# Spreading a row to all partitions through DRAM, and sixteen graphs written out, in a four-layer graph network on one core

## The reference, cut to what matters

```python
z = x @ W.T + bW
ai, aj = z @ wai + bai, z @ waj + baj          # one number for each node
e = ai + transpose(aj)                         # 1024 x 1024
e = where(e >= 0, e, 0.2 * e)
att = softmax(where(adjs > 0, e, -9e15) with a sink column of -1e9)[:, :n]
x = layernorm(x + att @ z)
```

## Time and profile before

| | |
|---|---|
| median of three executions | 3152.99 us |
| the profiled execution | 3149.12 us |
| its span, first to last instruction | 3147.0 us |
| PE busy (matmul) | 2898.2 us, 92% |
| DVE busy | 2090.7 us, 66% |
| ACT busy | 1324.8 us, 42% |
| POOL busy | 928.0 us, 29% |
| mean granted TensorE clock | 0.978 of full speed |

### The profile page before, as it was taken

The page is one execution under the profiler, slowest core; times in us unless marked ns, Lnnn a source line. Parts: engine busy times, 40 slices in busy tenths (PEclk is TensorE's granted clock), DMA queues, the critical chain, the costliest instruction groups (busy, mean ns, idle before and its releaser), DMA issues.

```text
span 3147.0 us, 45004 instructions
## 1 busy us (share of the span) xinstructions
PE 2898.2 (92%) x14794; PEld 2444.4 (78%) x14794; DVE 2090.7 (66%) x4724; ACT 1324.8 (42%) x2468; POOL 928.0 (29%) x1088
## 2 busy tenths in 40 slices
PE   4729999999999999999999999999999999999997
PEld 4618878887888878887888888888788878888886
DVE  3277677585867768585776758676676857677533
ACT  0232535435352533535253443526344362535423
POOL 1112332242233224232333323233332422332230
PEclk8969999999999999999999999999999999999998
DMA  4023040301304030120403012040302203040100
GB/s 130 19 89 100 1 134 1 108 28 41 94 1 134 1 108 27 44 91 1 134 1 115 20 50 86 5 130 1 122 14 71 64 13 123 1 134 1 37 18 14
DMA packets 203486, 181.41 MB, mean 58 GB/s; under 512 B 15568, under 2 KB 184944, under 8 KB 203248
## 3 DMA queue, kind: packets, MB, share of 16 engines
q1 hardware_dynamic: 62560, 109.94, 10.3%
q10 hardware_dynamic: 140688, 68.46, 7.8%
HBM read 161.17 MB, written 17.19 MB: 57 GB/s over the span
## 4 chain that ended last, share of the span: by engine, by line
PE 65%; issue 13%; DVE 7%; DMA 4%; POOL 3%; ACT 2%; SPq 1%; POOLq 0%; DVEq 0%; ACTq 0%
PE bank L716 18%; PE bank L732 16%; PE bank L673 8%; PE bank L675 8%; PE bank L674 8%; PE bank L632 2%; DMA adj_col<-in_adj 2%; PE bank L641 2%; DMA x_even<-in_x 2%; POOL rstd L1009 1%; DVE hid L1237 1%; DVE stat L1145 1%; PE bank L753 1%; PE bank L652 1%; POOL adj_col L1031 1%
## 5 line engine op out<-in xcount | busy, mean ns | idle before, releaser
L732 PE MATMUL bank<-W,hid 128*128 128x256 f32 x3072 | 696.7, 381 | 15.1 <-ACT hid L919 15.1
L732 PEld LDWEIGHTS bank<-W,hid 128*128 128x128 f32 x3072 | 580.7, 191 | 100.2 <-issue 18.7
L673 PE MATMUL bank<-mt_hi,x_hi 128*128 128x512 f32 x1536 | 639.2, 416 | 16.0 <-DVE mt_lo L1102 16.0
L675 PE MATMUL bank<-mt_hi,x_lo 128*128 128x512 f32 x1536 | 608.2, 396 | 0.0
L674 PE MATMUL bank<-mt_lo,x_hi 128*128 128x512 f32 x1536 | 605.4, 394 | 0.0
L849 ACT ACTIVATE mt_hi<-bank 128x512 fp32r<-128x512 f32 x512 | 278.9, 598 | 582.5 <-PE bank L641 549.2
L1226 DVE TENSOR_TENSOR sq_sum<-sq_sum,scratch 128x512 f32<-128x512 f32 x224 | 155.1, 692 | 376.9 <-ACT scratch L914 376.9
L1009 POOL TENSOR_TENSOR rstd<-ve,neg_half 128x4 f32<-128x4 f32 x128 | 129.9, 1015 | 921.8 <-DVE ve L1154 921.7
L1102 DVE TENSOR_TENSOR mt_lo<-bank,mt_hi 128x512 fp32r<-128x512 f32 x512 | 329.8, 685 | 77.7 <-ACT mt_hi L849 76.6
L673 PEld LDWEIGHTS bank<-mt_hi,x_hi 128*128 128x128 f32 x1536 | 293.5, 191 | 65.3 <-issue 17.4
L675 PEld LDWEIGHTS bank<-mt_hi,x_lo 128*128 128x128 f32 x1536 | 291.9, 190 | 65.0
(11 more groups left out here) (140 smaller groups left out, 4620.2 us busy)
## 6 DMA issues: line engine op xcount, KB each, us to landing
adj_col<-in_adj ACTq DMA_DIRECT2D x128, 512.0 KB, 3.9
att<-in_adj SPq DMA_DIRECT2D x128, 512.0 KB, 7.0
out<-x_even SPq DMA_DIRECT2D x64, 128.0 KB, 1.9
out<-x_odd SPq DMA_DIRECT2D x64, 128.0 KB, 1.9
x_even<-in_x SPq DMA_DIRECT2D x56, 128.0 KB, 4.4
x_odd<-in_x SPq DMA_DIRECT2D x56, 128.0 KB, 4.1
G<-in_L_gnn_W SPq DMA_DIRECT2D x2, 2560.0 KB, 14.1
W_f<-in_L_gnn_W SPq DMA_DIRECT2D x1, 1024.0 KB, 9.8
```

Of the source, the lines that this page charges most:

```text
L673: nc.tensor.matmul(dst[:], hi, mt_hi[:, k, cols], start=k == 0, stop=False)
L675: mm = nc.tensor.matmul(dst[:], lo, mt_hi[:, k, cols], start=False, stop=done and not extra)
L732: mm = nc.tensor.matmul(out_bank[t // 2][:, t % 2 * D:(t % 2 + 1) * D], src[:, t * P:(t + 1) * P], W2[:, m, :], start=(m == 0 and t % 2 == ...
```

## The change

1. The hardware loop is gone on all five engines: `for b in range(GRAPHS)` writes all sixteen graphs out with constant counts.
2. `aj_rows` on PE and `aj_copy` on DVE are gone. `attention_columns` writes aj and 0.2 aj side by side in a tile of 128 x 2 x 8. A new function `spread_aj` on SP waits for it, stores the 2048 numbers into an 8 KB tensor in DRAM (node order, so element by element), waits for that store, and loads it back with 8 KB for each of the 128 partitions, 1 MB in all, into `aj_rows`. It stands behind the loads of adjacency rows 4 to 7, and for graph 0 ahead of the first graph.
3. `scores(b, 0)` waits for that load in place of the two turn banks.
4. `hold` is gone.

```diff
-    aj_row, aj_row2 = sb("aj_row", [P, NODES]), sb("aj_row2", [P, NODES])
+    aj_rows = sb("aj_rows", [P, 2, NODES])
+    aj_flat = nc.dram_tensor("aj_flat", (2, NODES), F32, kind="Internal").ap()
...
+            def spread_aj(b, first=False):
+                sp.wait_ge(s_aj, b + 1)
+                with nc.allow_non_contiguous_dma(reason="columns to a row"):
+                    sp.dma_start(aj_flat.rearrange("a (t p) -> p a t", p=P), aj[:]).then_inc(s_aj_out, 16)
+                sp.wait_ge(s_aj_out, 16 * (b + 1))
+                if not first:
+                    sp.wait_ge(s_top, b * NT)
+                sp.dma_start(aj_rows[:], aj_flat.rearrange("(o a) n -> o a n", o=1).to_broadcast([P, 2, NODES]))\
+                  .then_inc(s_aj_in, 16)
...
                 if not last:
                     for k in range(4, NT):
                         load_row(b + 1, k)
+                    spread_aj(b + 1)
...
-            graph(0, 0, True, False)
-            with sp.Fori(0, GRAPHS // 2 - 1) as j:
-                graph(j * 2 + 1, 1, False, False)
-                graph(j * 2 + 2, 0, False, False)
-            graph(GRAPHS - 1, 1, False, True)
+            spread_aj(0, True)
+            for b in range(GRAPHS):
+                graph(b, b % 2, b == 0, b == GRAPHS - 1)
...
-                    elif k == 5 and not last:
-                        aj_rows(b + 1, False)
...
             def attention_columns(b):
-                nc.vector.tensor_scalar(aj[:], qj[:], c_cols[:, 1:2], None, ALU.add).then_inc(s_aj, 1)
+                nc.vector.tensor_scalar(aj[:, 0, :], qj[:], c_cols[:, 1:2], None, ALU.add).then_inc(s_aj_plain, 1)
                 nc.vector.tensor_scalar(ai[:], qi[:], c_cols[:, 0:1], None, ALU.add).then_inc(s_ai, 1)
+                dve.wait_ge(s_aj_plain, b + 1)
+                nc.vector.tensor_scalar(aj[:, 1, :], aj[:, 0, :], SLOPE, None, ALU.mult).then_inc(s_aj, 1)
...
                 if t == 0:
                     dve.wait_ge(s_shift, b + 1)
-                    for i in range(2):
-                        dve.wait_ge(s_turn_free[i], turn_aj_use(b) + 1)
+                    dve.wait_ge(s_aj_in, (b + 1) * 16)
...
                 if not last:
-                    aj_copy(b + 1)
                     scores(b + 1, 0)
                 agg_lo(b, 2, 0)
```

More of the change, by code:

```diff
@@ L476, in layers @@
     qi, qj = sb("qi", [P, NT]), sb("qj", [P, NT])
-    ai, aj = sb("ai", [P, NT]), sb("aj", [P, NT])
+    ai, aj = sb("ai", [P, NT]), sb("aj", [P, 2, NT])
     shift, floor = sb("shift", [P, NT]), sb("floor", [P, NT])
@@ L482, in layers @@
     ms, rms = sb("ms", [P, 2, 4]), sb("rms", [P, 2, 4])
-    held = sb("held", [P, 9])
     mvs = [mv0, mv, mv, mv3]
@@ L509, in layers @@
     s_cov = sem("bias_scaled")
+    s_aj_out, s_aj_in, s_aj_plain = sem("aj_written"), sem("aj_rows_loaded"), sem("aj_without_slope")
     s_sums, s_ai, s_aj, s_shift = sem("attention_sums"), sem("ai_columns"), sem("aj_columns"), sem("shift_and_floor")
@@ L517, in layers @@
     TURN_AT = {2: 4, 4: 5, 6: 6}
-    USES = 2 * NT + 1
+    USES = 2 * NT
     def turn_att_use(b, k):
-        return b * USES + 1 + k
-    def turn_aj_use(b):
-        return b * USES
+        return b * USES + k
     def turn_col_use(b, k):
-        return b * USES + 1 + NT + k
+        return b * USES + NT + k
     def hi_use(b, k, col):
@@ L642, in turn_col @@
                                                  adj_col[:, k % CR, 4 * i + j, :], ident[:])
-                    mm.then_inc(s_turned[i], 1)
-            def aj_rows(b, first):
-                pe.wait_ge(s_aj, b + 1)
-                for i in range(2):
[L648 to L653, removed]
                     mm.then_inc(s_turned[i], 1)
@@ L828, in graph @@
                     turn_att(b + 1, 7)
-            aj_rows(0, True)
             for k in range(NT):
                 turn_att(0, k)
[L833 to L837, removed]
+            for b in range(GRAPHS):
+                graph(b, b == 0, b == GRAPHS - 1)
             rms_sum(GRAPHS - 1, 1)
@@ L1092, in _ @@
         def _(dve):
-            def hold(place):
-                nc.vector.tensor_copy(held[:, place:place + 1], ones[:, 0:1])
             def turn_lo(b, k, col):
@@ L1103, in turn_lo @@
                                             ALU.subtract).then_inc(s_turn_free[i], 1)
[L1105 to L1111, removed]
             def agg_lo(b, layer, h):
@@ L1147, in statistics @@
                 dve.wait_ge(s_stats[layer], half_count(b, h))
-                hold(2 * layer + h)
                 for t in tiles(h):
@@ L1192, in scores @@
                 dve.wait_ge(s_mask, b * NT + t + 1)
-                nc.vector.scalar_tensor_tensor(out=own, in0=aj_row2[:], scalar=shift[:, t:t + 1],
-                                               in1=aj_row[:], op0=ALU.add, op1=ALU.max).then_inc(s_leaky, 1)
+                nc.vector.scalar_tensor_tensor(out=own, in0=aj_rows[:, 1, :], scalar=shift[:, t:t + 1],
+                                               in1=aj_rows[:, 0, :], op0=ALU.add, op1=ALU.max).then_inc(s_leaky, 1)
                 dve.wait_ge(s_leaky, b * NT + t + 1)
-                if t == 0:
-                    hold(8)
-                else:
+                if t > 0:
                     negated_top(b, t - 1)
@@ L1338, in _ @@
             attention_columns(0)
-            aj_copy(0)
             for t in range(NT):
```

## The result

| | before | changed |
|---|---|---|
| median, us (4 runs each) | 3153.45 (3152.75 to 3154.31) | 3307.14 (3306.17 to 3308.25) |
| ratio, 95% interval | | 1.0487 (1.0469 to 1.0506) |
| profiled execution, us | 3149.12 | 3306.17 |
| its span, granted clock | 3147.0, 0.978 | 3304.3, 0.949 |

The changed kernel is 154 us slower; the prediction said 32 us slower, with 3260 us as its upper end. PE is busy for slightly less time than before; what the kernel is longer by is idle time of PE. First the page of the changed kernel: its engines, and two of its costliest groups (busy us, mean ns, idle time ahead, and what ended it). The first line answers to the earlier trace rows.

The account below looks back on a forecast made before the run. PE, busy 92% of the span, was taken to bound the kernel. Turn ends -21, DVE work -3, late rows +32, clock +20, graph 0 +4 gave +32 us: median 3153 to 3185 us, range 3133 to 3260.

Parts of the forecast that it names:

- The store: SP's store of 2048 separate 4-byte numbers to DRAM: 3.5 us, bounds 1.9 and some 8 us.
- Rival 1: Storing scattered numbers, or broadcasting one 8 KB row to 128 partitions, is slow: 13 us chain, +106, 3259 us; chance 0.13.
- The load: SP's load of 1 MB from DRAM into aj_rows: 5.0 us, bounds 3.5 and 9.8 us.
- The chain: From aj ready through SP's DRAM write and read-back: 8.7 us; PE resumes 2.15 us later, 32 us over 15 graphs.
- The clock: PE at half clock after 3.9 us idle in nearly each graph: 1.3 us x 15 = 20 us, between 0 and 24.
- Graph 0: Ahead of the first scores, started at 185.03 before: they start at 188.7, 4 us later.
- Turn ends: Writing the loop out removes six loop turn ends of 3.5 us: 21 us saved, bounds 21 to 23.5.
- rival 3: Straight code is slower than the loop somewhere, so the 21 us stay: 3206 us; chance 0.02.
- Hold: On DVE, hold moves the next instruction by 0.07 us; its removal saves 0.2 us x 15 = 3 us, bounds 0 to 6.
- The removed matmuls and copies: PE's 16 matmuls, 1.75 us a graph, 26 us in 15, saved only if a_lo is not late; DVE's copies, 2.6 us.
- rival 2: The DRAM chain is short and the change a gain: at 6.4 us the sum is -14, 3139 us; chance 0.15.
- rival 2's lowest bounds: DRAM trips of 1.9 + 3.5 + 0.2 us: scores starts 0.6 us earlier, PE gains 0.3 us each graph, 3125 us.

Follow-up runs that it names:

- the first run: The kernel before with only its loops written out, in all five engines' programs: 3130.58 us, ratio 0.9929.
- the first two runs: One: kernel before with only its loops written out, 3130.58 us. Other: changed kernel with aj's row made by TensorE again, hold still gone, 3126.76 us.

## Why the prediction was wrong

The direction and the mechanism were right; the size was off by 122 us, and nearly all of that follows from one term, the store.

- **The store** was taken as 3.5 us, with 1.9 and 8 us as bounds, and took 11.0. The step that failed is "3.5 us between them": loads of scattered numbers stood in for a store of them. The 2.6 and 3.9 us of the loads did not carry over, since the store's price hangs on how close together it writes (4.1 us at 64 B, 11.0 us packed), and the upper bound, twice the load, had no row behind it. Rival 1 named the right cause, but its chain of 13 us had the same too low bound, so its 3259 us was too low as well.
- **The load** was taken as 5.0 us and took 4.7.
- **The chain** was to be 8.7 us and was 15.9. PE's delay grew with it one to one in graph 8, as the prediction had argued. From aj to the first hidden_tile it was 1752.98 - 1741.38 = 11.6 us before and is 1661.91 - 1641.03 = 20.9 us now; the difference of 9.3 us is the forecast's 2.15 and the 7.2 us by which the chain is longer. 15 x 7.2 = 108 us.
- **The clock** was to cost 1.3 us a graph. The window of 4.2 us at 0.50 holds ten matmuls that stood 0.43 us apart, where 0.23 is the distance at full clock (1666.33 to 1666.56 in the timeline above): 2.0 us in graph 8. Over the first 6 us behind the wait the clock is 0.55 to 0.74 in the fifteen graphs, 0.61 on average, which makes 2.3 us each, an estimate. So it cost 30 to 35 us in place of 20.
- **Graph 0** was to start its scores 4 us later and started them 10.8 us later, against the 185.03 of the earlier trace rows: 7 us more. PE felt it in full: its first transposes of attention in graph 0 start at 225.30, and at 214.60 in the kernel before. The timeline of DVE, the changed kernel, ahead of graph 0:

```profile
179.27 0.23 DVE L1148 TENSOR_SCALAR aj<-qj,c_cols 128x8 f32<-128x8 f32 x1
...
195.79 0.69 DVE L1165 TENSOR_SCALAR scratch<-att 128x1024 f32<-128x1024 f32 x1 [15.87 <-DMA aj_rows<-aj_flat]
```

- **Turn ends** were taken as 21 us (21 to 23.5) and were 23.4 by the first run. Straight code cost nothing that shows, so rival 3 was wrong. The idle time ahead of a graph's first aggregation is gone.
- **Hold** and the other small edits were taken as 3 us and were 3.8, the difference of the first two runs; their intervals overlap, so it may be nothing. From graph to graph it is 179.87 us with hold and 179.80 without (their profiled executions), 1 us in all.
- **The removed matmuls and copies** were argued to bring nothing as long as a_lo is late, and 26 us otherwise. The run with the rows of graph 0 alone confirms it: nothing is late there, and each graph is 1.9 us shorter, 28 us in all.

Summed again with the measured sizes: the chain 108, the clock 10 to 15, graph 0 7, turn ends and the small edits -3, so 3185 + 122 to 127 = 3307 to 3312 us, against 3307 measured. Another way round, from the run with the row by TensorE (3126.8 us): PE's new wait 163.6, the removed matmuls and copies -28, the half clock 30 to 35, graph 0 11; that makes 3303 to 3308 us.

Of the signs that the prediction named, the 15 waits of DVE and the idle time of PE with the clock at 0.50 behind them were there, at twice their size and more; "179 + 4 us from graph to graph" was 191.17, nearly alike in all graphs (190.8 to 191.5); "it is wrong if the store takes over 6 us" is what happened.

One sum of the prediction is wrong without bearing on the result. At rival 2's lowest bounds scores start 0.6 us earlier, and hold's 0.07 us comes on top, so a_lo ends at 1751.97 and PE, which is ready at 1751.23, gains 1.0 us in each graph and not 0.3; the 3125 us would have been some 3115.

The estimate of rival 2, 2.0 + 4.4 us for the two DMAs, is met nearly by rows of 64 B (1.4 + 4.6 us), and those gave 3134.54 us where rival 2 said 3139. The Trainium skill (DMA: Bandwidth & Descriptors, Anatomy of one DMA) gives that fit for DMAs issued by GpSimd, though, and both of these are issued by SP. The prediction's "the rows agree for 128 KB" was generous too: the fit makes 2.3 us of it, an estimate, and the earlier trace rows have 1.9. The Trainium skill (DMA: Bandwidth & Descriptors, Specifications) says that below 512 B a transfer misses line rate and becomes a read-modify-write. By that alone rows of 64 B would be slow too; here 128 of them took 1.4 us, and 16 rows of 512 B 1.3. The rule gave the right warning for separate numbers, but by the runs it is the separate writes close together that cost, not the size below 512 B alone.

## What to carry to other kernels

A DMA that sits in a wait chain counts from issue to the completion that someone waits for, and a store of separate small numbers that lie next to each other can take 8 times as long as the same bytes in rows: turn the data first, so that each write is a row. That made the store short, but the way by DRAM paid only once the work around it was put in a new order (1.3 us for the store in both runs, 3141.63 and 3102.03 us). A price that no row shows must not be bounded by its mirror image, a load for a store; where the sum hangs on it, the range has to be wide on that side. When a new wait is put on an engine, look at what is queued behind it, move what others wait for ahead of it, and then read again which wait ends last: here the second look was worth 40 us.

## What the runs showed of the hardware

Not expected was how a store of 4-byte numbers to DRAM behaves. At 64 or 32 B between two numbers it took 4 us for 2048 of them; at 16 B 5.4 us, at 8 B 9.4 us, packed 11.0 us, and 256 packed numbers still took 7.7 us. In the packed case the packets had left the DMA engines after 2.5 us and the completion came 8.5 us later. So most of the time passes where the profile shows no work of the DMA engines. It is set more by how close the writes lie than by how many there are: an eighth of the numbers, equally packed, saved 3.3 us (11.0 to 7.7), while the same 2048 at 32 B in place of 4 B saved 7.2 us (11.0 to 3.8). The number of packets does not decide it: 64 B apart and packed have the same 97888. That writes into one line wait for each other is my inference from these times; no row shows the memory's side. Open are the size of such a line (1 and 2 numbers per 64 B took the same time, so 32 B and 64 B both fit), why 8 numbers 8 B apart took nearly as long as 16 packed ones and 1.4 us longer with the runs of 8 spread over 128 KB, and why the load behind some of these stores took up to 6.2 us in place of 4.7.
